# First routed layer of even token tiles: a GpSimd copy out of on-chip memory, or a DMA from DRAM issued by SP

## The reference

```
h = relu(x @ Wi.T + bi)                                # 2048 x 256
for l in 0, 1:
    shared = h @ Ws[l].T + bs[l]
    routed = h @ Wr[l, e].T + br[l, e]                 # e = route_id of the token's group of 32 tokens, 16 experts
    h = relu(shared + routed + h)
out = h @ Wo.T + bo
```

## Time and profile before

| | us |
|---|---|
| median of 3 runs | 646.8 (645.96 to 648.7) |
| the profiled execution: its own time | 647.73 |
| the profiled execution: span of the trace | 646.0 |
| routed stage in it: first first-layer matmul to the last output matmul's end | 551.97 to 639.6 |
| VectorE busy | 512.5 (79%) |
| TensorE busy | 551.0 (85%) |
| GpSimd busy | 173.5 (27%) |

### The profile page before, as it was taken

The page is one execution under the profiler, slowest core; times in us unless marked ns, Lnnn a source line. Parts: engine busy times, 40 slices in busy tenths (PEclk is TensorE's granted clock), DMA queues, the critical chain, the costliest instruction groups (busy, mean ns, idle before and its releaser), DMA issues.

```text
span 646.0 us, 13284 instructions
## 1 busy us (share of the span) xinstructions
PE 551.0 (85%) x5082; PEld 430.6 (67%) x5082; DVE 512.5 (79%) x907; ACT 372.4 (58%) x756; POOL 173.5 (27%) x186
## 2 busy tenths in 40 slices
PE   1978792999999999899998899899996846999985
PEld 0668782687775878775784666568886645566753
DVE  6499979895788767599939827999999899999520
ACT  1699693668876767775857735552331301566463
POOL 4211114021012100895441100031214000365741
PEclk9979895889998989998998989899999788899998
DMA  6477750021165065899599205020201944465750
GB/s 138 94 136 142 194 121 2 11 73 41 61 212 196 18 212 193 178 214 236 106 217 125 72 2 197 2 65 1 66 1 49 305 137 143 125 210 172 204 166 17
DMA packets 48857, 78.36 MB, mean 121 GB/s; under 512 B 5406, under 2 KB 24870, under 8 KB 48794
## 3 DMA queue, kind: packets, MB, share of 16 engines
q1 hardware_dynamic: 30714, 52.02, 25.3%
q0 software_dynamic: 15488, 22.02, 20.2%
q10 hardware_dynamic: 2592, 3.48, 1.9%
HBM read 80.61 MB, written 22.06 MB: 159 GB/s over the span
## 4 chain that ended last, share of the span: by engine, by line
PE 50%; DVE 26%; ACT 14%; issue 5%; DMA 2%; POOL 1%; SPq 1%; ACTq 1%; DVEq 0%
DVE arena L1620 16%; PE bank L687 13%; PE bank L699 10%; PE bank L616 10%; PE bank L852 5%; ACT arena L1130 5%; PE bank L813 2%; ACT maskT L995 2%; DVE arena L1445 2%; ACT ysb L1078 2%; PE bank L565 1%; PE bank L592 1%; DMA routed_sums<-in_wsT 1%; PE bank L797 1%; PE bank L601 1%
## 5 line engine op out<-in xcount | busy, mean ns | idle before, releaser
L486 POOL TENSOR_TENSOR x<-x,ysb 128x512 f32<-128x512 f32 x36 | 75.7, 2104 | 248.9 <-ACT ysb L1078 245.9
L1130 ACT ACTIVATE arena<-heads,nd 128x512 bf16<-128x512 f32 x176 | 112.1, 726 | 22.8 <-PE bank L616 22.8
L687 PE MATMUL bank<-hTc,arena 128*128 128x512 f32 x192 | 96.7, 660 | 5.6 <-ACT reg_c L1067 5.6
L1620 DVE SCALAR_TENSOR_TENSOR arena<-reg_b,nd,arena 128x1536 f32<-128x1536 f32 x48 | 92.0, 1977 | 0.0
L699 PEld LDWEIGHTS bank<-arena,reg_c 128*128 128x128 f32 x768 | 87.6, 192 | 4.8 <-issue 4.7
L699 PE MATMUL bank<-arena,reg_c 128*128 128x128 f32 x768 | 88.5, 275 | 0.0
L1067 ACT ACTIVATE reg_c<-bank,b 128x512 f32<-128x512 f32 x96 | 65.3, 687 | 26.6 <-PE bank L687 26.6
L616 PEld LDWEIGHTS bank<-reg_b,arena 128*128 128x128 bf16 x1536 | 75.3, 101 | 5.8 <-DVE arena L1478 2.9
L616 PE MATMUL bank<-reg_b,arena 128*128 128x99 bf16 x1536 | 76.5, 213 | 2.7 <-DVE arena L1478 2.7
L1464 DVE TENSOR_TENSOR arena<-maskT,arena 128x2048 bf16<-128x2048 bf16 x36 | 50.9, 1414 | 31.4 <-ACT arena L1130 31.4
L687 PEld LDWEIGHTS bank<-hTc,arena 128*128 128x128 f32 x192 | 39.4, 211 | 53.3 <-issue 44.9
(11 more groups left out here) (195 smaller groups left out, 865.4 us busy)
## 6 DMA issues: line engine op xcount, KB each, us to landing
maskT<-routed_sums SPq DMA_DIRECT2D x48, 256.0 KB, 3.3
reg_c<-in_adj POOLq DMA_DIRECT2D x16, 512.0 KB, 7.7
arena<-in_w1T SPq DMA_DIRECT2D x16, 512.0 KB, 3.9
arena<-in_w2T SPq DMA_DIRECT2D x16, 512.0 KB, 4.8
routed_sums<-in_wsT SPq DMA_DIRECT2D x32, 256.0 KB, 5.5
routed_sums<-in_wrT POOLq DMA_DIRECT2D x32, 256.0 KB, 13.5
arena<-routed_sums SPq DMA_DIRECT2D x32, 256.0 KB, 3.0
routed_sums<-ident POOLq DMA_DIRECT2D x4, 1024.0 KB, 12.4
```

The costliest lines, as they stand in the source:

```text
L486: nc.gpsimd.tensor_tensor(xi, xi, ysb[:, e % 3, :].rearrange("p (t d) -> p t d", d=P), ALU.add).then_inc(s_acc, 1)
L687: mm(bank[b][:, :], w1[:, s, e % 2, c * P:(c + 1) * P], hTc[:, :], start=True, stop=True).then_inc(full[b], 1)
L1130: last = af(ind[:, q, b, j, :], sbc[:, h, :], ACT.Relu, bias=nd[:, q * QT + j, h:h + 1], scale=BIG)
L1620: last = v.scalar_tensor_tensor(p, row, nd[:, t, h:h + 1], p if h else maskT[:, t, columns], ALU.max, ALU.mult)
```

## The change

SP now loads the first-layer weights of even tiles 2, 4, ..., 14 straight from DRAM into the same four slots, 4 DMAs of 256 KB a tile, each with its read of the expert number. They stand in SP's list between second-layer loads. GpSimd's `select` is gone, and so is its wait for the kept matrices. SP still loads the kept matrices, and ScalarE still copies the odd tiles' from them. `s_even` counts DMA completions, 16 each.

```diff
@@ block.sync
             load_second(0)
             load_second(1)
-            for t in range(4, T):
-                sp.wait_ge(full[3 + t % 2 * 2], (BANK5 if t % 2 else BANK3) + (t - 4) // 2 * (L + 1) + L)
-                load_second(t)
+            for t in range(2, T, 2):
+                sp.wait_ge(full[3], BANK3 + (t - 2) // 2 * (L + 1) + 1)
+                for g in range(GT):
+                    e = sp.value_load(route[0:1, t * GT + g:t * GT + g + 1], min_val=0, max_val=E1 - 1)
+                    sp.dma_start(w_first[:, g, :, :].unsqueeze(1),
+                                 routed[:, 0, bass.ds(e, 1), :].rearrange("p o (k n) -> p o k n", k=KC)
+                                 ).then_inc(s_even, 16)
+                for n in (t + 2, t + 3) if t + 2 < T else ():
+                    sp.wait_ge(full[3 + n % 2 * 2], (BANK5 if n % 2 else BANK3) + (n - 4) // 2 * (L + 1) + L)
+                    load_second(n)
@@ block.gpsimd
-            def select(t):
-
-                pool.wait_ge(full[3], BANK3 + (t - 2) // 2 * (L + 1) + 1)
-                for g in range(GT):
-                    e = pool.value_load(route[0:1, t * GT + g:t * GT + g + 1], min_val=0, max_val=E1 - 1)
-                    last = nc.gpsimd.tensor_copy(w_first[:, g, :, :].rearrange("p k n -> p (k n)").unsqueeze(1),
-                                                 kept[:, bass.ds(e, 1), :])
-                last.then_inc(s_even, 1)
-
             one_hot(0)
             one_hot(1)
-            pool.wait_ge(s_kept, 16 * E1)
             for c in range(C):
...
                 for i in range(CT):
-                    if i % 2 == 0 and c * CT + i + 2 < T:
-                        select(c * CT + i + 2)
                     pool.wait_ge(ev["y"], FFN_Y + c * CT + i + 1)
@@ block.tensor, layer(t, l)
                 if l == 0 and t < 2:
                     pe.wait_ge(s_pair, 16 * 2 * GT)
+                elif l == 0 and t % 2:
+                    pe.wait_ge(s_odd, t // 2)
                 elif l == 0:
-                    pe.wait_ge(s_odd if t % 2 else s_even, t // 2)
+                    pe.wait_ge(s_even, 16 * GT * (t // 2))
```

More of the change, by code:

```diff
@@ L233, in gnn_moe_stack @@
         s_pair = sem("first_pair_of_routed_tiles_loaded")
-        s_even = sem("even_tile_weights_selected")
+        s_even = sem("even_tile_weights_loaded")
         s_odd = sem("odd_tile_weights_selected")
```

## The result

The changed kernel takes 663.34 us in the median of 4 runs (661.01 to 664.03), the kernel before 647.36 us (645.96 to 648.7, 4 runs). The ratio is 1.0244, 95% interval 1.0222 to 1.0267: 16.0 us slower. The forecast was 659.3, +12.5 us on a median of 646.8. The profiled execution of the changed kernel is the fastest of its four, 661.01 us with a span of 659.2, 13.3 us above the profiled one of before.

The account below looks back on a forecast made before the run. TensorE and ScalarE taking turns bound the routed stage; after the change SP's queue would in short pairs. Late weights +11.6 us and clock +0.9 gave +12.5 on 646.8, so 659.3 us; range 654 to 665.

Parts of the forecast that it names:

- What bounds: Routed stage: TensorE and ScalarE take turns before the change, 9.5 to 14.5 us a pair; SP's queue added, 13.7 us.
- The removed copies at nothing: Routed stage: removing GpSimd's 28 copies, on no path, is worth 0, bounds 0 to -0.5 us.
- SP's step: SP's queue, routed stage: issue to issue with the expert number's read takes 1.14 us, bounds 1.10 and 1.20.
- The table of pairs: Even tiles 2 to 14: first-layer weights arrive late, delays growing from 0 to 11.6 us at tile 14.
- The clock: TensorE after tile 14's wait: slower clock adds 0.9 us, bounds 0 and 1.8.
- The bounds of the terms: Whole kernel: the forecast's range with its terms' bounds, 656 to 663 us.
- the wider range: Whole kernel: 654 to 665 us, meant to hold the time 8 times in 10.
- steps at the upper bound: Rival, SP's queue: steps of 1.20 us, +16.1 us, with the clock 664 to 665 us; 17%.
- Landing: SP's loads in the routed stage: landing stays at 3.0 us median, bounds 2.7 and 5.
- The page's rule: SP's issues in the routed stage: by it they cost little, transfers bound, no change at 646.8 us; rival, 6%.

Follow-up runs that it names:

- half bytes: Changed kernel with half of each even tile's first-layer matrix not loaded, all 28 reads and issues kept: 660.94 us, ratio 1.0205 to the kernel before.
- half issues: Changed kernel with even tiles' first-layer loads as 14 DMAs of 512 KB instead of 28 of 256 KB, reads halved too: 650.01 us, ratio 1.0046.
- the first trace: Profiled execution of the changed kernel, the fastest of its first four runs: 661.01 us, span 659.2.
- the other order: Changed kernel with first-layer loads of tile t placed between second-layer loads of tiles t and t+1 on SP: 659.38 us, ratio 1.0183.
- the second trace: Changed kernel run again without edit; the trace is of the longest of five runs, span 665.0, stretch 95.38.
- the second set: Changed kernel run again without edit, 5 runs: median 661.25 us (660.86 to 666.87), ratio 1.0211 to the kernel before.
- the kernel with odd copies on GpSimd: Changed kernel with SP's expert numbers read ahead and reused for both layers, plus odd tiles' copies moved from ScalarE to GpSimd: 647.56 us, ratio 1.0002.

## Why the prediction was right

**What bounds.** Right: a ping-pong of TensorE and ScalarE, and after the change SP's queue in the short pairs. Three readings of the trace of before were off and changed nothing in the sum. Tile 0's row names no releaser; ScalarE's L1283 released the other seven. In the routed stage the attention matmuls (L813) run from 565.1 to 609.3, that is in pairs 2/3 to 8/9 and not up to 10/11. And SP's 8 loads a pair are 9.2 us at 1.156 each, not 9.1.

**The removed copies at nothing.** Right, shown by leaving them out (0.9995). VectorE was faster and idle, as argued.

**SP's step.** The mechanism held in each of its parts: issues and not bytes (half bytes against half issues), the read as half of the step (0.52 us without, 1.10 with one, 1.64 with two), ordinary steps of 1.10 us for the loads into `reg_c` (3.64 less 0.34, over 3). The size was off: 1.14 was the forecast for the mean, 1.167 and 1.19 are what two traces have. Over 75 steps that is 2.0 and 3.7 us, nearly all of the stretch's excess: +11.6 was forecast, +13.7 and +15.6 measured.

The term that was too small is mostly the 1.10 us for the new loads. It came from a run of eight in the earlier trace rows that has no long step. With the steps that lead to them and the long ones, the 27 steps to loads into `reg_c` have a mean of 1.163 us in the first trace and 1.191 in the second; that alone is 1.7 and 2.5 us. Of the 75 steps, 8 and 10 are long, 1.34 to 1.91 us. Some hold a long read or a long issue; in the first trace the longest read and the longest issue are (ns min/median/max):
```profile
L409 SPq TENSOR_LOAD <-route x28: 263/269/937, 552.4 to 639.6; - x28
...
L410 SPq DMA_DIRECT2D reg_c<-routed_sums x28: 337/338/628, 553.1 to 640.6; - x28
```
But the 11th, 32nd, 54th and 75th step are long in both traces, at 1.43 to 1.46 us, with ordinary reads and issues. The 11th of the first trace:
```profile
564.23 0.34 SPq L397 DMA_DIRECT2D arena<-routed_sums  x1
...
565.67 0.35 SPq L397 DMA_DIRECT2D arena<-routed_sums  x1
```
They are long in the traces of half the bytes and of the other order too, so these go with the place in SP's list and not with chance. What makes a step long was not tried and stays open.

**The table of pairs.** Right in its pattern: tiles 4, 6, 12 and 14 late, the long pairs catching up. Counted from the start of tile 0, tile 4 starts 1.2 us later than before, tile 6 5.3, tile 8 6.6, tile 10 6.6, tile 12 9.1 and tile 14 13.7 (forecast 1.3, 4.7, 5.3, 5.3, 7.4 and 11.6). At tile 8 a DMA wait was forecast, the trace has none: TensorE's own pair took 14.31 us instead of 13.00, as its clock was down after the wait at tile 6 (first layer 1.96 us instead of 1.09). So part of the delay at tile 8 came another way than forecast.

**The clock.** +0.9 us with bounds 0 to 1.8; 1.18 and 2.23 in the two tails, the second beyond the bound. In the first trace the clock fell only after tile 14's first layer, the one that was reckoned slow; in the second it was down over the first layers of both tiles, 1.96 us each. With the stretch this makes 14.9 and 17.8 us, which brackets the 16.0 of the medians.

**What the number owes.** The bounds of the terms gave 656 to 663, and 663.34 is just above them, within the wider range. The rival "steps at the upper bound" reckoned +16.1 us for the stretch, with 90 us for the 75 steps; the second trace has 89.2 and +15.6. The median of 663.34 lies nearer to that rival (664 to 665) than to the forecast, and the 661.25 of the second set lies between the two: same mechanism, longer steps.

**Landing.** Right at 3.1 us in the median for this kernel (3.0 forecast). Landing of loads of 256 KB rose in the median (3.8 to 4.0 us) only where steps were 0.5 us.

**The page's rule.** By the Trainium skill, "DMA: Bandwidth & Descriptors", section "Issuing engines are not separate DMA queues", the time to initiate a DMA is usually small beside the transfer. Here one load took 3.1 us to land, but landings overlap and the steps on SP don't. What compares with the step of 1.167 us is the transfer's share of the engines' time, 0.84 us (the prediction's estimate, from 279 GB/s at a share of 0.89). The step was the larger, and moving 28 loads to an engine whose queue then had no pause left cost 16 us.

## What to carry to other kernels

Price a DMA by the step from issue to issue on its engine, with the read of its address, and compare the queue's total per round with the round; a queue that idles for 20 us over a stage, as SP's did here, may still have no room for half as much again. In such a queue put what is due first ahead, and keep indices in registers when they are used twice. A copy that is hidden on an idle engine is worth nothing when removed; ask instead which copies stand between two engines that take turns.

## What the runs showed that was not expected

GpSimd can be held up for the whole of a train of VectorE's products. In the kernel with odd copies on GpSimd, VectorE ran products from 561.39 to 572.1 without a gap, and a copy of 0.61 us took 9.27. In the second trace of the changed kernel a cast, which took 0.87 us in the first trace, took 10.51:
```profile
576.28 10.51 POOL L519 CAST routing<-onehot 128x512 bf16<-128x512 f32 x1
```
beside VectorE's
```profile
575.64 2.73 DVE L1617 SCALAR_TENSOR_TENSOR arena<-hT,nd,maskT 128x512 f32<-128x512 f32 x4
578.29 5.38 DVE L1617 SCALAR_TENSOR_TENSOR arena<-hT,nd,arena 128x512 f32<-128x512 f32 x8
583.59 2.73 DVE L1617 SCALAR_TENSOR_TENSOR arena<-ysb,nd,arena 128x512 f32<-128x512 f32 x4
```
VectorE runs at its 0.68 us each all the while. When the copies got in, as in the earlier trace rows at 579.25, both slowed: the copies to 1.0 us each, VectorE's eight products from 580.67 on to 7.54 us instead of 5.38. The Trainium skill, "SBUF — State Buffer", section "SBUF: two separate sides", says that the two share a port pair as an exclusive lock, which an operation of VectorE with two inputs in SBUF holds for the whole instruction against a GpSimd operation that reads SBUF. The traces agree with one holding up the other, and go further: here GpSimd was held up for 9 to 10 us over a train of such instructions, not for one instruction's 0.7. What decides between being held up and taking turns, no run here shows.
